# A Perceiver, RWKV and switched-attention layer on one core: the low parts of the transposed context blocks made by adding transfers instead of by VectorE and GpSimd

## The chip, the core and the metric

The kernel runs on one core of a Trainium2 chip. The metric is the device time of one execution in microseconds (us). TensorE (PE in the rows) multiplies matrices, and its weight loads are listed as PEld; VectorE is DVE, ScalarE is ACT, GpSimd is POOL, and SyncE (SP) issues transfers. Each engine works through its own list of instructions in order and waits on semaphores for the others; 16 DMA engines move data between device memory and the on-chip memory (SBUF). TensorE accumulates into eight banks of PSUM.

## The reference

Inputs are x (2 x 128 x 512) and a context (2 x 2048 x 512), all float32. There are three layers, each added to x after a layer norm. The first holds the change: self-attention, then a cross-attention over the context, then a small feed-forward part. The cross-attention is

```
Q = x @ Wq;  K, V = (context @ Wk, context @ Wv)
energy = einsum('bqd,bkd->bqk', Q, K)            # b = 2, q = 128, k = 2048
lengths = sum(energy[:, 0] != 0)                 # keys beyond the length are masked
score = softmax(where(pad, -inf, energy) / sqrt(32))
out = einsum('bqk,bkd->bqd', score, V)
```

The second layer is one RWKV-7 block with a state that starts at zero (eight projections, sigmoid and softplus gates, group norm); the third is an eight-head attention with experts chosen by the top two of five gates.

## The kernel before

The kernel never forms K and V of the whole context. It folds Wk into the query (`Q @ Wk.T`, called k2) and multiplies the result by the transposed context, and it gathers the context with the softmax weights before it multiplies by Wv (v2). So the context is read twice: in eight transposed blocks `ct00` to `ct13` (batch 0 or 1, quarter 0 to 3 of the keys) for the energies, and in eight plain blocks `c00` to `c13` for the gather. Each block is 128 x 2048 float32, 1 MB.

These sixteen products are made from rounded operands (float32r, which TensorE reads faster) in three passes so that precision is kept: each operand is split into a rounded high part and a low part, which is the remainder, and the product is high x high + low x high + high x low. The function `three` does that with 12 matmuls of 128 x 512 a block. The split of a context block has these steps:

- SyncE loads the block into its place in `ring` (`fetch`, L306). There are nine places for all weights and blocks (PLACE, L24), and a new block waits until the product that read the old one is done.
- ScalarE (`split`, L1333) writes the high part into one of the three places 9 to 11. Block i takes the place of block i - 3, so its split waits until the product of that block is done.
- VectorE (`low`, L806) writes block minus high part over the block for columns 0 to 1407, and GpSimd (`low`, L1578) does so for the other 640 columns. The two work at the same time, each after the split.
- TensorE waits in `three` for the split and both low parts.

The lists of all engines are written out by hand. TensorE's order around the change is: the self-attention of both batches, the query products q2(0) and k2(0), then scores(0,0), (0,1), (0,2), (0,3), q2(1), a count of nonzero energies, k2(1), scores(1,0), two transposes of the softmax weights of batch 0, scores(1,1) and (1,2), two more transposes, scores(1,3), and then the four gathers of batch 0 and the four of batch 1. VectorE counts nonzero energies after each of the scores (`nonzero`, L887) and makes the masked maximum of a batch (`maxima`, L900) once its count is through TensorE (`length2`, L892). GpSimd's list also holds the power -0.5 of every layer norm (`deviation`, L1574), on which the norm on VectorE waits; two of these, for x1 of both batches, stand between the low parts of `ct02` and `ct03`.

Of the kernel before, what the change touches and what calls it, by code (L numbers as in the profile page):

```python
# [7 lines left out]
ALU = mybir.AluOpType  # L8
ACT = mybir.ActivationFunctionType
# [5 lines left out]
BLOCKS = ["q1", "k1", "v1", "q2", "k2", *[f"ct{b}{n}" for b in range(2) for n in range(4)],  # L15
          "c00", "c01", "c02", "c03", "v2", "c10", "c11", "c12", "c13", "f1", "f2",
          "rk", "ra", "rw", "rr", "rv", "rg", "ro", "rf", "fg", "fq", "fk", "fo"]
# [6 lines left out]
PLACE = {n: i % 9 for i, n in enumerate(BLOCKS[:24])}  # L24
# [3 lines left out]
SPLITS = [f"ct{b}{n}" for b in range(2) for n in range(4)] + [f"c{b}{n}" for b in range(2) for n in range(4)]  # L28
# [47 lines left out]
def build(nc, blocks, xin, vecs, cols, out):  # L76
    with ExitStack() as ctx:
# [3 lines left out]
        def sem(name):  # L81
            return ctx.enter_context(nc.semaphore(name))
# [7 lines left out]
        ring = view("ring", [128, PLACES, 2048], F32, at)  # L90
        ring_r = view("ring_r", [128, PLACES, 2048], F32R, at)
# [54 lines left out]
        def high(name):  # L146
            return 9 + SPLITS.index(name) % 3
# [60 lines left out]
        def flags(name, *orders):  # L208
            return [Flag(sem(f"{name}{b}"), orders[b if len(orders) > 1 else 0]) for b in range(2)]
# [3 lines left out]
        four = ["0", "1", "2", "3"]  # L213

        s_place = [sem(f"s_place{p}") for p in range(PLACES)]
        s_x = [sem("s_x0"), sem("s_x1")]
        s_cols, s_bc0, s_bc1, s_bc2 = (sem(n) for n in ("s_cols", "s_bc0", "s_bc1", "s_bc2"))
        s_y = [sem("s_y0"), sem("s_y1")]
# [2 lines left out]
        own_v = Steps(sem("dve_steps"))  # L221
        var = flags("var_and_eps", LNS)
        normed = flags("normed", LNS)
        split_low = Flag(sem("split_low_dve"), SPLITS)
        energy_in = flags("energy_read", ["n1", "len1", "nb1", "max1", "pT"])
        k1_in = flags("k1_in", ["k1"])
        turned_v = Flag(sem("x_turned_dve"), ["x1"])
# [18 lines left out]
                      ["q1", "v1", "q2", "k2", "pc", "relu", "k", "th", "w", "r", "v", "g"])  # L246
        exped = flags("exped", ["e1"] + four)
        split_high = Flag(sem("split_high"), SPLITS)
        p_high = flags("p_high", four)
        mixed = flags("mixed", ["a", "k", "v", "r", "g"], ["w", "g"])  # L250
        sq_a = flags("squared", ["vc"], ["kx", "a", "wexp", "y"])
# [8 lines left out]
        own_g = Steps(sem("pool_steps"))  # L260
        const = Flag(sem("constants"), ["mhalf", "ident", "ones", "kidx", "causal", "kof", "top", "wbias", "tri", "sel"])
        rstd = flags("rstd", LNS)
        split_lowg = Flag(sem("split_low_pool"), SPLITS)
        x2b_g = flags("x2b", ["x2b"])
        mixed_g = Flag(sem("mixed_pool"), ["w", "g"])
        rk_g = flags("rwkv_pool", ["sb", "sc", "pv"], ["kx", "c2", "a", "c3", "sb", "w", "c1", "pv", "rs"])
# [107 lines left out]
        def _(eng):  # L374
# [36 lines left out]
            def three(o_, xs, name, first, last):  # L411

                s.wait_ge(*split_high.at(name))
                s.wait_ge(*split_low.at(name))
                s.wait_ge(*split_lowg.at(name))
                ws = [ring_r[:, p, :].rearrange("p (c n) -> p c n", c=4) for p in (high(name), PLACE[name])]
                pairs = [(xs[0], ws[0]), (xs[1], ws[0]), (xs[0], ws[1])]
                for n, (x, w) in enumerate(pairs):
                    for c in range(4):
                        i = mm(o_, x(c), w[:, c, :], first and n == c == 0, last and n == 2 and c == 3)  # L420
                return i
# [359 lines left out]
        def _(eng):  # L781
# [24 lines left out]
            def low(name):  # L806
                p = PLACE[name]
                s.wait_ge(*split_high.at(name))
                v.tensor_tensor(ring_r[:, p, 0:CUT], ring[:, p, 0:CUT], ring_r[:, high(name), 0:CUT],  # L809
                                ALU.subtract).then_inc(*split_low.inc(name))  # L810
# [340 lines left out]
            weigh(0)  # L1151
            pT(0)
            k1_out(1)
            low("ct00")
            low("ct01")
            add1(0)
            energies(1)
            low("ct02")
            norm1(0)
            lengths(1)  # L1160
            masked(1)
# [5 lines left out]
            norm1(1)  # L1167
            k2_split(0)
            nonzero(0, 0)
            low("ct03")  # L1170
            nonzero(0, 1)
            low("ct10")
            nonzero(0, 2)
            low("ct11")
            nonzero(0, 3)
            low("ct12")
            length2(0)
            maxima(0)
            k2_split(1)
# [1 line left out]
            guard(0, len2[0])  # L1181
            weigh2(0)
            nonzero(1, 0)
            low("ct13")
            p_split(0, 0)
            p_split(0, 1)
            nonzero(1, 1)
# [146 lines left out]
        def _(eng):  # L1334
            s = Waits(eng)

            def act(o, x, func, **kw):
                return a.activation(o, x, func, **kw)  # L1338
# [9 lines left out]
            def split(name):  # L1348
                i = SPLITS.index(name)
                s.wait_ge(*loaded(name))  # L1350
                if i > 2:
                    s.wait_ge(*used(SPLITS[i - 3]))
                act(ring_r[:, high(name), :], ring[:, PLACE[name], :], ACT.Copy).then_inc(*split_high.inc(name))

            def exp1(b):
                em = slots[:, 16, 256 + b * 128:384 + b * 128]
# [214 lines left out]
        def _(eng):  # L1571
# [6 lines left out]
            def low(name):  # L1578
                p = PLACE[name]
                s.wait_ge(*split_high.at(name))  # L1580
                g.tensor_tensor(ring_r[:, p, CUT:], ring[:, p, CUT:], ring_r[:, high(name), CUT:],  # L1581
                                ALU.subtract).then_inc(*split_lowg.inc(name))

            def mul(o, x, y, flag, name, op=ALU.mult):
                g.tensor_tensor(o, x, y, op).then_inc(*flag.inc(name))  # L1585

# [22 lines left out]
            g.affine_select(out=tri[:, :, :], in_=tri[:, :, :], compare_op=ALU.is_gt, fill=0.0, base=0,  # L1609
                            pattern=[[1, 5], [-1, 5]], channel_multiplier=0).then_inc(*const.inc("tri"))  # L1610
            deviation(1, "x")
            low("ct00")
            low("ct01")
            low("ct02")
            deviation(0, "x1")
            deviation(1, "x1")
            for name in SPLITS[3:]:
                low(name)
            for b in range(2):
                deviation(b, "x2")  # L1620
# [130 lines left out]
```

## Time and profile before

| | before |
|---|---|
| median of 3 runs | 277.52 us (277.33 to 278.31) |
| span of the profiled execution, first to last instruction | 275.8 us |
| mean granted clock of TensorE in it | 0.937 of full speed |
| busy: TensorE, its weight loads | 237.3 us (86%), 167.4 us (61%) |
| busy: VectorE, ScalarE, GpSimd | 177.9 us (64%), 88.3 us (32%), 99.6 us (36%) |

The profile gives no duration of the profiled execution other than its span; the part outside the span is taken as the difference to the median, 1.7 us. The table's shares are means over the whole span. The work in question lies between 23 and 123 us of it.

### The profile page before, as it was taken

How to read it: one execution, taken by the hardware profiler on the slowest of the kernel's cores; microseconds unless marked ns; L12 is line 12 of the kernel's file. 1: busy time of each engine (PE TensorE's matmuls, PEld its weight loads, DVE VectorE, ACT ScalarE, POOL GpSimd, SP SyncE). 2: the span in 40 equal slices, each digit the busy share in tenths (PEclk: the TensorE clock that was granted, in tenths of full speed). 3: DMA queues.
4: the chain of work that ended last, by engine and by line, in shares of the span. 5: the costliest groups of instructions: out<-in, count | busy, mean ns of one | idle time of the engine just before them, and what ended most of it. 6: DMA issues, size and time to landing. Idle time of an engine off the chain costs nothing.

```text
span 275.8 us, 3044 instructions
## 1 busy us (share of the span) xinstructions
PE 237.3 (86%) x1133; PEld 167.4 (61%) x1133; DVE 177.9 (64%) x327; ACT 88.3 (32%) x151; POOL 99.6 (36%) x82
## 2 busy tenths in 40 slices
PE   6999869899599949999989999970987599996995
PEld 5969458789488727677554444430433279895952
DVE  2236953379658999540747559599646869899360
ACT  2106410363467538412014545410202302321110
POOL 4002810088039933530402024886215236160000
PEclk9999968999899997999999999997799979999579
DMA  6999991002799991009800797000000000000001
GB/s 269 394 421 450 409 422 76 1 0 101 289 429 421 421 424 51 0 11 392 358 2 1 221 421 311 1 0 0 0 0 0 2 0 0 4 0 0 2 37 40
DMA packets 6350, 43.98 MB, mean 159 GB/s; under 512 B 832, under 2 KB 832, under 8 KB 1472
## 3 DMA queue, kind: packets, MB, share of 16 engines
q1 hardware_dynamic: 6336, 43.80, 39.1%
q8 instruction: 9, 0.15, 0.2%
q14 instruction: 5, 0.04, 0.1%
HBM read 43.27 MB, written 0.52 MB: 159 GB/s over the span
## 4 chain that ended last, share of the span: by engine, by line
PE 54%; DVE 29%; POOL 5%; issue 5%; ACT 4%; DMA 1%; DVEq 0%; POOLq 0%; ACTq 0%
PE psum L378 50%; PE psum L382 4%; DVE ring_r L809 4%; ACT slots L1338 3%; POOL small L1576 3%; DVE slots L1078 3%; DVE slots L904 2%; POOL slots L1585 2%; DVE slots L1081 2%; DVE small L785 1%; DVE slots L978 1%; DVE slots L909 1%; DMA slots<-xin 1%; DVE small L1091 1%; DVE slots L998 1%
## 5 line engine op out<-in xcount | busy, mean ns | idle before, releaser
L378 PE MATMUL psum<-ring,slots 128*128 128x512 f32 (+3 forms) x228 | 96.2, 576 | 4.4 <-ACT slots L1338 4.4
L378 PEld LDWEIGHTS psum<-ring,slots 128*128 128x128 f32 (+1 forms) x228 | 43.2, 209 | 48.7 <-issue 41.5
L1338 ACT ACTIVATE slots<-psum 128x512 f32<-128x512 f32 (+3 forms) x51 | 27.7, 552 | 123.6 <-PE psum L378 76.2
L1581 POOL TENSOR_TENSOR ring_r<-ring,ring_r 128x640 fp32r<-128x640 f32 x16 | 41.5, 2608 | 48.5 <-ACT ring_r L1338 48.5
L378 PE MATMUL psum<-slots,ring 128*128 128x128 f32 x448 | 54.7, 283 | 2.9 <-ACT slots L1338 2.4
L378 PEld LDWEIGHTS psum<-slots,ring 128*128 128x128 f32 x448 | 53.5, 199 | 5.1 <-ACT slots L1338 3.4
L378 PE MATMUL psum<-ring_r,slots_r 128*128 128x512 f32 x192 | 48.4, 410 | 3.4 <-issue 3.4
L378 PEld LDWEIGHTS psum<-ring_r,slots_r 128*128 128x128 f32 x192 | 37.1, 196 | 12.6 <-issue 4.9
L1576 POOL TENSOR_TENSOR small<-small,mhalf 128x1 f32<-128x1 f32 x16 | 14.9, 932 | 62.2 <-DVE small L789 62.2
L1338 ACT ACTIVATE ring_r<-ring 128x2048 fp32r<-128x2048 f32 (+1 forms) x17 | 31.7, 1864 | 14.2 <-PE psum L378 12.6
L382 PE MATMUL psum<-ident,slots 128*128 128x128 f32 x104 | 17.1, 298 | 19.5 <-DVE slots L1274 7.9
L809 DVE TENSOR_TENSOR ring_r<-ring,ring_r 128x1408 fp32r<-128x1408 f32 x16 | 29.8, 1871 | 6.1 <-ACT ring_r L1338 6.1
L382 PEld LDWEIGHTS psum<-ident,slots 128*128 128x128 f32 x104 | 13.2, 152 | 26.4 <-DVE slots L1274 8.7
L1338 ACT ACTIVATE slots<-slots,small 128x128 f32<-128x128 f32 (+1 forms) x30 | 12.7, 476 | 11.8 <-DVE small L915 6.5
L785 DVE BATCH_NORM_STATS2 small<-slots 128x6 f32<-128x512 f32 x16 | 11.1, 693 | 5.0 <-DMA slots<-xin 4.6
L1585 POOL TENSOR_TENSOR slots<-slots 128x512 f32<-128x512 f32 x7 | 9.3, 1335 | 13.7 <-ACT slots L1338 13.5
L1585 POOL TENSOR_TENSOR slots<-slots,bc 128x512 f32<-128x512 f32 x7 | 9.7, 1392 | 4.5 <-DVE slots L998 2.6
L1338 ACT ACTIVATE slots_r<-psum 128x512 fp32r<-128x512 f32 (+1 forms) x11 | 5.9, 558 | 16.7 <-PE psum L378 8.5
L803 DVE SCALAR_TENSOR_TENSOR slots<-slots,small,bc 128x512 f32<-128x512 f32 x10 | 7.5, 752 | 5.7 <-POOL small L1576 5.7
L935 DVE SCALAR_TENSOR_TENSOR slots<-psum,small,slots 128x512 f32<-128x512 f32 x2 | 1.5, 750 | 12.2 <-PE psum L378 12.2
L378 PE MATMUL psum<-slots 64*128 64x128 f32 (+2 forms) x68 | 8.7, 303 | 0.6 <-DVE slots L864 0.4
L978 DVE SCALAR_TENSOR_TENSOR slots<-slots,colv 128x128 f32<-128x128 f32 x16 | 6.5, 458 | 3.1 <-PE psum L378 3.0
(149 smaller groups left out, 211.1 us busy)
## 6 DMA issues: line engine op xcount, KB each, us to landing
ring<-blocks SPq DMA_DIRECT2D x36, 1024.0 KB, 10.2
bc<-vecs SPq DMA_DIRECT2D x1, 3072.0 KB, 28.4
bc<-vecs SPq DMA_DIRECT2D x1, 1280.0 KB, 8.1
slots<-xin SPq DMA_DIRECT2D x2, 256.0 KB, 3.9
bc<-vecs SPq DMA_DIRECT2D x1, 512.0 KB, 9.9
y<-slots SPq DMA_DIRECT2D x2, 256.0 KB, 2.0
colv<-cols SPq DMA_DIRECT2D x1, 14.0 KB, 8.7
```

Of the source, the lines that this page charges most:

```text
L378: return t.matmul(o_, l, r, start=first, stop=last)
L382: i = t.transpose(o_[:, c * 128:(c + 1) * 128], x[:, c * 128:(c + 1) * 128], ident[:, :])
L785: v.bn_stats(st[b], x).then_inc(*own_v.inc())
L803: v.scalar_tensor_tensor(out=o, in0=tmp, scalar=rs[b], in1=vec(bname), op0=ALU.mult, op1=ALU.add).then_inc(*normed[b].inc(name))
L809: v.tensor_tensor(ring_r[:, p, 0:CUT], ring[:, p, 0:CUT], ring_r[:, high(name), 0:CUT], ALU.subtract).then_inc(*split_low.inc(name))
L904: v.tensor_scalar(PT[b][:, at_], kidx[:, :], low4[b][:, n:n + 1], NEG, ALU.is_ge, ALU.mult).then_inc(*own_v.inc())
L978: i = v.scalar_tensor_tensor(out=dst[:, c, :], in0=bcols(T10, 1)[:, c, :], scalar=colv[:, 4 * k + c:4 * k + c + 1], in1=bcols(T8, 1)[:, c, ...
L1078: v.tensor_tensor(heads(N4[b] if first else Y[b]), x_, w_, ALU.mult).then_inc(*own_v.inc())
L1338: return a.activation(o, x, func, **kw)
L1576: g.tensor_tensor(rs[b], ve[b], mhalf[:, 0:1], ALU.pow).then_inc(*rstd[b].inc(name))
L1581: g.tensor_tensor(ring_r[:, p, CUT:], ring[:, p, CUT:], ring_r[:, high(name), CUT:], ALU.subtract).then_inc(*split_lowg.inc(name))
L1585: g.tensor_tensor(o, x, y, op).then_inc(*flag.inc(name))
```

## The change

For the eight transposed blocks the remainder is no longer computed by VectorE and GpSimd. ScalarE runs a second activation over the block in place: it overwrites the block with minus its rounded value. Then GpSimd's queue issues a transfer of the same block from device memory onto that place with an add as its write operation, so that block + (-rounded) is left there. TensorE waits for that transfer (16 increments of a semaphore for each block) instead of the two low parts. The eight `low` calls go from VectorE's list and the eight from GpSimd's; the plain blocks c00 to c13 are split as before.

```
+        s_added = {n: sem(f"s_added_{n}") for n in SPLITS[:8]}
...
                 s.wait_ge(*split_high.at(name))
-                s.wait_ge(*split_low.at(name))
-                s.wait_ge(*split_lowg.at(name))
+                if name.startswith("ct"):
+                    s.wait_ge(s_added[name], 16)
+                else:
+                    s.wait_ge(*split_low.at(name))
+                    s.wait_ge(*split_lowg.at(name))
...
             k1_out(1)
-            low("ct00")
-            low("ct01")
             add1(0)
             energies(1)
-            low("ct02")
             norm1(0)
...
                 act(ring_r[:, high(name), :], ring[:, PLACE[name], :], ACT.Copy).then_inc(*split_high.inc(name))
+                if i < 8:
+                    s.wait_ge(*split_high.at(name))
+                    act(ring_r[:, PLACE[name], :], ring[:, PLACE[name], :], ACT.Copy, scale=-1.0).then_inc(
+                        *minus_high.inc(name))
...
+            def add_block(name):
+
+                s.wait_ge(*minus_high.at(name))
+                g.dma_start(ring_r[:, PLACE[name], :], blocks[BLOCKS.index(name), :, :], accum_op=ALU.add).then_inc(
+                    s_added[name], 16)
...
             deviation(1, "x")
-            low("ct00")
-            low("ct01")
-            low("ct02")
+            add_block("ct00")
+            add_block("ct01")
+            add_block("ct02")
             deviation(0, "x1")
             deviation(1, "x1")
-            for name in SPLITS[3:]:
+            add_block("ct03")
+            add_block("ct10")
+            add_block("ct11")
+            add_block("ct12")
+            add_block("ct13")
+            for name in SPLITS[8:]:
                 low(name)
```

The diff also takes the calls of `low` for ct03 and ct10 to ct13 from between the counts on VectorE.

ScalarE's list, from the exponent of batch 0's self-attention on; `ring_r<-ring 128x2048` is a pass over a whole context block. Before:

```order
4 L1338 ACTIVATE slots,small<-slots,small 128x128
5 L1338 ACTIVATE ring_r<-ring 128x2048 x2
6 L1338 ACTIVATE slots<-psum 128x4x128
7 L1338 ACTIVATE ring_r<-ring 128x2048
8 L1338 ACTIVATE slots<-psum 128x512
```

And after the change:

```order
4 L1335 ACTIVATE slots,small<-slots,small 128x128
5 L1335 ACTIVATE ring_r<-ring 128x2048 x4
6 L1335 ACTIVATE slots<-psum 128x4x128
7 L1335 ACTIVATE ring_r<-ring 128x2048 x2
8 L1335 ACTIVATE slots<-psum 128x512
```

The eviction of q1 of batch 1 (row 6) now stands behind four passes instead of two. Further down the same list, from the split of ct03 to the first evictions of softmax weights (`slots_r<-psum 128x512`), before:

```order
14 L1338 ACTIVATE ring_r<-ring 128x2048 x4
15 L1338 ACTIVATE slots<-psum 128x4x128
16 L1338 ACTIVATE slots_r<-psum 128x4x128
17 L1338 ACTIVATE slots,small<-slots,small 128x512 x4
18 L1338 ACTIVATE ring_r<-ring 128x2048
19 L1338 ACTIVATE slots_r<-psum 128x512 x2
```

And after the change:

```order
14 L1335 ACTIVATE ring_r<-ring 128x2048 x8
15 L1335 ACTIVATE slots<-psum 128x4x128
16 L1335 ACTIVATE slots_r<-psum 128x4x128
17 L1335 ACTIVATE slots,small<-slots,small 128x512 x4
18 L1335 ACTIVATE ring_r<-ring 128x2048 x2
19 L1335 ACTIVATE slots_r<-psum 128x512 x2
```

The split of ct13 (row 18) is now two passes, ahead of the evictions of row 19. GpSimd's list from the second deviation on, before:

```order
21 L1576 TENSOR_TENSOR small<-small,mhalf 128x1
22 L1581 TENSOR_TENSOR ring_r<-ring,ring_r 128x640 x3
23 L1576 TENSOR_TENSOR small<-small,mhalf 128x1 x2
24 L1581 TENSOR_TENSOR ring_r<-ring,ring_r 128x640 x13
25 L1576 TENSOR_TENSOR small<-small,mhalf 128x1
```

And after the change:

```order
21 L1577 TENSOR_TENSOR small<-small,mhalf 128x1
22 L1588 DMA ring_r<-blocks 128x2048 x3
23 L1577 TENSOR_TENSOR small<-small,mhalf 128x1 x2
24 L1588 DMA ring_r<-blocks 128x2048 x5
25 L1582 TENSOR_TENSOR ring_r<-ring,ring_r 128x640 x8
26 L1577 TENSOR_TENSOR small<-small,mhalf 128x1
```

The deviations of x1 now stand behind three issues of adding transfers, each of which waits for ScalarE's second pass.

## Rows read from the trace of the kernel before

**Rows 1.** The page's first two parts, whole span.
```profile
PE 237.3 (86%) x1133; PEld 167.4 (61%) x1133; DVE 177.9 (64%) x327; ACT 88.3 (32%) x151; POOL 99.6 (36%) x82
...
PEclk9999968999899997999999999997799979999579
```

**Rows 2.** The chain that ended last: start us, us, what.
```profile
50.98 14.82 PE psum L378 x80
...
70.96 2.36 issue
73.32 4.58 PE psum L378 x12
...
78.77 5.50 PE psum L378 x24
...
94.57 1.73 DVE slots L904
...
102.54 0.16 DVE small L915
```

**Rows 3.** Timeline, 54:62: start us, us, engine, what [idle before <-releaser].
```profile
53.79 8.43 PE L378 MATMUL psum<-ring_r,slots_r 128*128 128x512 f32 x36
...
54.05 1.92 ACT L1338 ACTIVATE ring_r<-ring 128x2048 fp32r<-128x2048 f32 x1 [2.49 <-PE psum L378]
...
56.00 1.62 DVE L809 TENSOR_TENSOR ring_r<-ring,ring_r 128x1408 fp32r<-128x1408 f32 x1 [1.33 <-ACT ring_r L1338]
56.05 8.82 POOL L1581 TENSOR_TENSOR ring_r<-ring,ring_r 128x640 fp32r<-128x640 f32 x3 [7.10 <-ACT ring_r L1338]
```

**Rows 4.** The low parts' durations in ns, min/median/max.
```profile
L1581 POOL TENSOR_TENSOR ring_r<-ring,ring_r x16: 1543/2960/3028, 25.0 to 112.3; 128x640 fp32r<-128x640 f32 x16
```

**Rows 5.** All 36 block transfers, from issue to landing.
```profile
DMA to landing us min/median/max: 4.6/10.2/30.4
```

**Rows 6.** Issues by line, 0 to 50 us: KB each, median us to landing.
```profile
ring<-blocks SPq DMA_DIRECT2D x12, 1024.0 KB, 13.5
```

**Rows 7.** Stretches: us, busy us of each engine, PEclk, DMA share, GB/s.
```profile
38.00:41.00 3.00, 2.75 (x13) 2.75 (x14) 0.74 (x4) 0.58 (x3) 0.00 (x0) 0.50 1.00 415
...
57.00:60.00 3.00, 3.00 (x15) 2.34 (x14) 2.51 (x4) 2.20 (x2) 3.00 (x2) 1.00 0.00 0
...
78.00:84.00 6.00, 6.00 (x32) 5.06 (x30) 4.46 (x8) 4.80 (x4) 3.39 (x2) 1.00 1.01 426
```

**Rows 8.** Timeline of SyncE, its first issue of a block: start us, us.
```profile
1.23 0.42 SPq L312 DMA_DIRECT2D ring<-blocks  x1
```

**Rows 9.** Timeline, 20 to 41 us.
```profile
27.81 0.60 ACT L1338 ACTIVATE slots<-psum 128x512 f32<-128x512 f32 x1 [0.38 <-PE psum L378]
...
32.81 2.73 POOL L1576 TENSOR_TENSOR small<-small,mhalf 128x1 f32<-128x1 f32 x1 [0.47 <-DVE small L789]
...
36.45 1.11 PE L382 MATMUL psum<-ident,slots 128*128 128x128 f32 x4 [3.09 <-DVE slots L803]
...
38.25 6.08 PE L378 MATMUL psum<-slots,ring 128*128 128x128 f32 x32 [0.69 <-ACT slots L1338]
```

**Rows 10.** Timeline, 62 to 73 us, from q2(1) to scores(1,0).
```profile
62.06 3.73 PE L378 MATMUL psum<-slots,ring 128*128 128x128 f32 x32
...
66.46 1.32 DVE L897 TENSOR_SCALAR small<-kof,small 128x4 f32<-128x4 f32 x1
...
72.53 0.68 DVE L884 TENSOR_TENSOR slots_r<-psum,slots_r 128x512 fp32r<-128x512 f32 x1
```

**Rows 11.** Timeline, 77 to 88 us, around scores(1,3).
```profile
77.99 1.92 ACT L1338 ACTIVATE ring_r<-ring 128x2048 fp32r<-128x2048 f32 x1 [1.75 <-PE psum L378]
...
83.63 5.95 POOL L1581 TENSOR_TENSOR ring_r<-ring,ring_r 128x640 fp32r<-128x640 f32 x2 [0.62 <-ACT ring_r L1338]
84.10 1.03 PE L382 MATMUL psum<-ident,slots 128*128 128x128 f32 x8
...
84.89 5.73 PE L378 MATMUL psum<-ring_r,slots_r 128*128 128x512 f32 x24
```

More of the change, by code:

```diff
@@ L223, in build @@
         normed = flags("normed", LNS)
-        split_low = Flag(sem("split_low_dve"), SPLITS)
+        split_low = Flag(sem("split_low_dve"), SPLITS[8:])
         energy_in = flags("energy_read", ["n1", "len1", "nb1", "max1", "pT"])
@@ L248, in build @@
         split_high = Flag(sem("split_high"), SPLITS)
+        minus_high = Flag(sem("minus_high"), SPLITS[:8])
         p_high = flags("p_high", four)
@@ L262, in build @@
         rstd = flags("rstd", LNS)
-        split_lowg = Flag(sem("split_low_pool"), SPLITS)
+        split_lowg = Flag(sem("split_low_pool"), SPLITS[8:])
         x2b_g = flags("x2b", ["x2b"])
@@ L1169, in _ @@
             nonzero(0, 0)
-            low("ct03")
             nonzero(0, 1)
-            low("ct10")
             nonzero(0, 2)
-            low("ct11")
             nonzero(0, 3)
-            low("ct12")
             length2(0)
@@ L1183, in _ @@
             nonzero(1, 0)
-            low("ct13")
             p_split(0, 0)
```

## The prediction

> **What bounds the kernel now.** I read the page first, then the chain that ended last, then the timeline around each of the eight transposed blocks, then stretches with the granted clock. The shares say that TensorE is busy 86% of the span and VectorE 64% [rows 1]. The chain says more: from 50.98 to 65.8 us it is TensorE without a break (scores of batch 0, then q2 of batch 1), and again from 77.9 to 84.3; only later, from 84 to 103 us, does VectorE hold it [rows 2]. So in the stretch in which the eight blocks are used, what counts is whether a block is ready when TensorE comes to it. VectorE and GpSimd have slack there, and time taken off them is worth something only where the chain runs through them. The reader should also see in rows 1 that among the first 17 clock digits (6.9 us each) there are three clear drops; each follows an idle gap of TensorE of 3 us or more.
>
> **Part 1: what is removed.** Eight low parts on VectorE (1.62 us each at best, as the row at 56.00) and eight on GpSimd, of 1.54 to 3.03 us, median 2.96 [rows 3, 4]. That is at least 13 us of VectorE and between 12 and 24 us of GpSimd. Nearly all of it lies beside TensorE's work. It is on the chain, or lengthens what is on it, at two places only, named below.
>
> **Part 2: what is added.** For each block a second ScalarE pass of 1.92 us [rows 3], then an issue on GpSimd's queue, then the landing of an adding transfer. These three come one after the other, where the two low parts ran side by side behind the first pass. The trace has no adding transfer. Let D be the time from the end of the second pass to its landing. From below: the fastest landing of a plain 1 MB block is 4.6 us [rows 5]; an adding one cannot well be shorter, as it moves the same bytes and reads the place too. From above: a block in the first 50 us, which queues behind others, takes 13.5 us in the median [rows 6]; with 2.5 us more for the second read (1 MB at 421 GB/s [rows 7]) that is 16 us. I take, for a quiet moment, 4.6 + 2.5 + 0.4 for the issue (SyncE's first took 0.42 us [rows 8]) = 7.5 us, near the lower row because the DMA engines are idle at 57 to 60 us [rows 7]. For ct13, which is added in the midst of the load stream (DMA share 1.01 [rows 7]), half the rate would make it 12.5; I take 10.
>
> The Trainium skill, "Collectives: The Full Stack" (why AllGather, ReduceScatter and AllReduce differ), holds that an adding transfer is slowed by its two source reads and not by the addition, and gives 62.28 against 32.35 GB/s, a factor of 1.93. By that a 2.5 us move would be an estimated 4.8 us, which is D = 7.3 in place of 7.5; no run here shows it yet.
>
> **Part 3: the first three blocks (23 to 41 us).** They are not needed before 50.98 us, so even at 16 us their adding transfers are covered: ScalarE runs 23.0 to 26.9 for ct00, to 30.7 for ct01, then the eviction of q1 of batch 1 (27.81 before [rows 9]), then ct02 until 35.2; 35.2 + 16 = 51.2. But two things are queued behind. The eviction comes 2.9 us later, and so do e1 and v1 of batch 1 on TensorE, which have slack to about 36 us. And GpSimd's deviation of x1 of batch 0 stands behind the issue of ct02's add, which waits for 35.2: it ends about 37.2 instead of 35.5, although VectorE, freed of two low parts, would have been ready for it some 2 us sooner than before. It was 2.73 us long, since it shared its time with a low part of VectorE, and would now be about 1 [rows 9]. The norm, and q2(0) behind it, come 1.7 us later. Against that TensorE's gap ahead of them shrinks from 3.1 to about 2 us, because v1 of batch 1 now fills it. If the clock then stays up, q2(0) takes 3.8 instead of 6.08 us (the row at 62.06 is the same work at full clock [rows 9, 10]) and the transposes 0.7 instead of 1.11: -2.7. Bounds -1.0 and +1.7; I take +0.5.
>
> **Part 4: ct03.** Its high part can be written only when scores(0,0) is done: 54.05 to 55.97. Before, both low parts were there at 59.0 (56.05 + 2.96), and TensorE reached scores(0,3) at 53.79 + 2 x 2.81 = 59.4, just in time [rows 3]. Now the second pass ends at 57.9 and the block is there at 57.9 + 7.5 = 65.4: a stall of 6.0 us. The gap lowers the clock: scores(1,0), which follows a gap of 3.0 us, took 4.58 us against 2.81, so +1.8 for scores(0,3) [rows 2, 3]. Two things come back. Behind q2(1) the chain runs over the maxima of batch 0 on VectorE; there the 128x4 instruction of L897 took 1.32 us while GpSimd still worked on a low part, and without it about 0.2: -1.1 [rows 10]. And since k2(1) keeps its length while VectorE comes sooner, the gap ahead of scores(1,0) falls from 3.0 to 1.7 us; I count the clock as kept, -1.8. Sum of the part: 6.0 + 1.8 - 1.1 - 1.8 = +4.9 (bounds at D = 4.6 and 16: +0.2 without the drop of the clock, and +13.4). ct10, ct11 and ct12 are added 15 us and more before they are needed, and cost nothing.
>
> **Part 5: ct13.** Its high part waits for scores(1,0), which ends at 77.9. Passes 77.99 to 81.8 [rows 11]; landing at 81.8 + 10 = 91.8. TensorE wants it at 84.9 [rows 11]: 6.9 us, and again +1.8 for the clock, +8.7 (bounds at D = 4.6 and 16: +1.5 and +14.7). The evictions of batch 0's weights come 1.9 us later behind the second pass, and with them the low parts of the weights on VectorE, but the next transposes wait only at 83.9 and are just met. Behind scores(1,3) the order is as before: split of c02, low parts of c02 and c03, maxima of batch 1. GpSimd has the same low parts there, so the slowed instructions of L904 (1.73 us at 94.57 [rows 2]) stay. From there the delay is carried to the end unchanged.
>
> **Sum.** 0.5 + 4.9 + 8.7 = 14.1 us on a span of 275.8; with 1.7 us outside the span the median goes from 277.5 to 291.6. I say 291.
>
> **Rivals.** *The transfers are hidden and the freed engines pay.* VectorE and GpSimd slow each other where both work: a GpSimd low part takes 1.54 us at its shortest and 2.96 in the median [rows 4]. If the adds land in 4.6 us, part 3 gives -1.0, ct03 +0.2, ct13 +1.5, and if GpSimd, no longer late with ct13, is out of the way of batch 1's maxima (94.5 to 102.5 us, 8.0 long, against 67.8 to 72.5, or 4.7, for the same work in batch 0 [rows 2, 10]), another -3.3: -2.6, 274.9 us, faster. It decides below D = 5.9 or so for both blocks. Against it: a landing equal to the very fastest plain one, from a queue that has not been used in this kernel.
>
> *The adding transfer is slow*, 16 us: 0.5 + 13.4 + 14.7 = 28.6, 306 us. For it: 16384 elements an engine have to pass whatever adds them, and nothing in the trace says how fast.
>
> *The issue on GpSimd is long.* If it takes 3 us, as a low part beside VectorE does [rows 4], instead of 0.4, all three places slip by 2.6: 14.1 + 7.8 = 21.9, 299 us. The two engines wait for each other in the rows above. The Trainium skill, "SBUF — State Buffer" (the "DVE blocks DMA" trap), says the same of transfers issued from GpSimd: their descriptors cannot be written while a VectorE instruction holds the shared port pair. By that rule the sum would move toward this rival only where VectorE works long, and at 57.9 and 81.8 it now has only short instructions.
>
> *The change adds up to nothing*: D near 6 at both places, 277.5.
>
> **Chances.** Forecast 0.50 (283 to 297), long issue 0.15, slow adder 0.22, hidden 0.08, nothing 0.05. The range of 282 to 307 leaves out the last two and a tail of about 0.06 above. Half a percent (1.4 us) is about what a measurement of this kernel can tell from no change: faster 0.08, same 0.05, slower 0.87.
>
> **What would show it.** In the changed profile: ScalarE has eight more 1.92 us passes; TensorE idles ahead of scores(0,3), with a releaser that is a transfer, for about 6 us, and ahead of scores(1,3) for about 7; the clock falls behind each; the first three blocks cause no stall; q2(0) starts near 40 us; L897 of batch 0 takes 0.2 us. I am wrong if there is no idle time ahead of scores(0,3), if the adds take under 6 us or over 16 from the end of the pass, or if ct10 to ct12 stall TensorE too.

## The result, and the profile after

| | before | after |
|---|---|---|
| median | 277.42 us (275.56 to 278.31, 4 runs) | 295.26 us (293.17 to 296.38, 4 runs) |
| ratio, 95% interval | | 1.0639 (1.0563 to 1.0714), slower |
| profiled execution | span 275.8 us | 296.38 us, span 294.6 us |

The changed kernel is slower by 17.8 us. The forecast was 291 us, with a range of 282 to 307. In all tables the medians are of all runs, and the ratios leave out the runs that took over 1.5% longer than the fastest of the same kernel. The page after, in the same order of engines as [rows 1], with the groups that the change touches (line engine op, tile, count | busy, mean ns | idle before them and what ended most of it; q0 is the queue of GpSimd's transfers, with packets, MB and share of the 16 engines):

```profile
PE 241.7 (82%) x1133; PEld 169.3 (57%) x1133; DVE 160.6 (55%) x319; ACT 102.8 (35%) x159; POOL 84.3 (29%) x82
...
PEclk9999999978999579689999999999589979999579
...
q0 software_dynamic: 1152, 8.39, 14.1%
...
L380 PE MATMUL psum<-ring_r,slots_r 128*128 128x512 f32 x192 | 52.4, 431 | 19.3 <-DMA ring_r<-blocks 17.1
...
L1335 ACT ACTIVATE ring_r<-ring 128x2048 fp32r<-128x2048 f32 (+1 forms) x25 | 46.6, 1874 | 27.0 <-PE psum L380 25.2
...
L1588 POOL DMA_DIRECT2D ring_r<-blocks x8 | 7.2, 894 | 62.1 <-ACT ring_r L1335 62.1
...
ring_r<-blocks POOLq DMA_DIRECT2D x8, 1024.0 KB, 12.8
```

The change does what it says: VectorE is 17.3 us less busy, GpSimd 15.3 less, ScalarE 14.5 more. The fourth row holds the answer: of 19.3 us that TensorE idled ahead of these products, a transfer into `ring_r` ended 17.1. The chain that ended last (start us, us, what), beside [rows 2]:

```profile
53.26 1.93 ACT ring_r L1335
55.20 1.92 ACT ring_r L1335
...
57.41 7.99 DMA ring_r<-blocks
65.54 8.14 PE psum L380 x44
73.69 10.53 DMA ring<-blocks
84.25 1.93 ACT ring_r L1335
86.20 1.92 ACT ring_r L1335
88.40 12.38 DMA ring_r<-blocks
100.92 5.47 PE psum L380 x12
...
113.05 1.73 DVE slots L909
```

Where [rows 2] had TensorE without a break, the chain now leaves it twice: two passes, the issue, the landing of the adding transfer, once for ct03 and once for ct13, the second time behind the plain load of ct13 itself (10.53 us). The timeline (start us, us, engine, what, idle before and its releaser), beside [rows 3, 9, 10, 11]:

```profile
39.68 3.84 PE L380 MATMUL psum<-slots,ring 128*128 128x128 f32 x32 [0.69 <-ACT slots L1335]
...
50.17 5.71 PE L380 MATMUL psum<-ring_r,slots_r 128*128 128x512 f32 x24 [0.47 <-issue]
...
56.27 3.01 PE L380 MATMUL psum<-ring_r,slots_r 128*128 128x512 f32 x12 [0.40 <-DMA ring_r<-blocks]
57.41 0.89 POOL L1588 DMA_DIRECT2D ring_r<-blocks  x1 [9.29 <-ACT ring_r L1335]
65.54 4.55 PE L380 MATMUL psum<-ring_r,slots_r 128*128 128x512 f32 x12 [6.26 <-DMA ring_r<-blocks]
74.21 0.23 DVE L902 TENSOR_SCALAR small<-kof,small 128x4 f32<-128x4 f32 x1
79.98 3.01 PE L380 MATMUL psum<-ring_r,slots_r 128*128 128x512 f32 x12 [1.56 <-ACT slots_r L1335]
84.25 3.86 ACT L1335 ACTIVATE ring_r<-ring 128x2048 fp32r<-128x2048 f32 x2 [1.34 <-DMA ring<-blocks]
87.15 2.97 PE L380 MATMUL psum<-ring_r,slots_r 128*128 128x512 f32 x12 [0.52 <-DMA ring_r<-blocks]
88.40 0.86 POOL L1588 DMA_DIRECT2D ring_r<-blocks  x1 [13.20 <-ACT ring_r L1335]
100.92 8.33 PE L380 MATMUL psum<-ring_r,slots_r 128*128 128x512 f32 x24 [9.93 <-DMA ring_r<-blocks]
```

Read beside before, this gives the shift of each point. The difference of two neighbours is what the stretch between them costs.

| point | before | after | shift |
|---|---|---|---|
| k1 of batch 1, ahead of any changed work | 20.25 | 22.26 | +2.0 |
| scores(0,0) starts | 50.98 | 50.17 | -0.8 |
| scores(0,2) starts | 56.6 | 56.27 | -0.3 |
| scores(0,3) starts | 59.4 | 65.54 | +6.1 |
| scores(0,3) ends | 62.2 | 70.1 | +7.9 |
| scores(1,0) starts | 73.32 | 79.98 | +6.7 |
| scores(1,0) ends | 77.9 | 83.0 | +5.1 |
| scores(1,3) starts | 84.9 | 100.92 | +16.0 |
| scores(1,3) ends | 87.7 | 106.4 | +18.7 |
| last instruction | 275.8 | 294.6 | +18.8 |

The first row is not the change's. The first projections took 8.85 us in this execution against 7.41 before, and the same happens in kernels that leave this stretch alone (8.84 us in the one with three low parts later, 7.41 in the one with two). Up to 11 us the matmuls come at 7 a us and then at 12, as if at half and at full clock, but the granted clock is shown as 1.00 in both stretches, so the reason stays open. By 56 us it is swallowed: scores(0,2) begins when ct02 has landed, at 56.1. In the kernel without ct13, which does not lose this time and starts scores(0,0) at 48.76, scores(0,2) begins at 56.05 as well. (59.4, 62.2, 56.6 and 87.7 are places inside a row of before, by 2.81 us for each block of 12 matmuls.)

The eight issues and landings, and three stretches with the busy us of PE, PEld, DVE, ACT and POOL, the granted clock, the DMA share and GB/s:

```profile
DMA to landing us min/median/max: 8.0/12.8/20.2
```

```profile
57.40:61.20 3.80, 1.88 (x9) 1.20 (x7) 0.69 (x2) 3.77 (x3) 0.93 (x2) 1.00 0.65 123
61.20:65.40 4.20, 0.00 (x0) 0.00 (x0) 0.00 (x0) 3.37 (x2) 1.32 (x2) 0.61 0.96 197
...
70.00:73.70 3.70, 3.70 (x34) 3.58 (x32) 0.69 (x2) 3.48 (x2) 0.00 (x0) 1.00 1.04 215
...
100.90:106.40 5.50, 5.48 (x13) 4.34 (x14) 0.00 (x0) 0.00 (x0) 0.00 (x0) 0.50 1.01 426
```

When the transfer of ct03 is issued, the last plain loads take about one more microsecond, and it lands 8.0 us after its issue. From 70.0 to 73.7 us the engines are as full as with plain loads and move 215 GB/s, where a plain stream moves 426. The last row is scores(1,3) at half clock behind the idle time.

### The profile page after: what moved, and what is told of

Read it like the earlier page. It is cut to its first block, busy times and chain, and to the rows that moved or that the text cites. A ratio compares the mean times of both kernels' runs of the same rounds, so it can differ in the third digit from the quotient of the medians.

```text
span 294.6 us, 3042 instructions
## 1 busy us (share of the span) xinstructions
PE 241.7 (82%) x1133; PEld 169.3 (57%) x1133; DVE 160.6 (55%) x319; ACT 102.8 (35%) x159; POOL 84.3 (29%) x82
## 3 DMA queue, kind: packets, MB, share of 16 engines
q0 software_dynamic: 1152, 8.39, 14.1%
## 4 chain that ended last, share of the span: by engine, by line
PE 45%; DVE 23%; DMA 11%; ACT 10%; POOL 5%; issue 4%; DVEq 0%; POOLq 0%; ACTq 0%
PE psum L380 42%; ACT ring_r L1335 7%; DMA ring_r<-blocks 7%; PE psum L384 4%; DMA ring<-blocks 4%; ACT slots L1335 3%; DVE slots L1083 2%; POOL small L1577 2%; POOL slots L1592 2%; DVE slots L1086 1%; DVE slots L909 1%; DVE small L790 1%; DVE ring_r L814 1%; DVE slots L983 1%; DVE slots L914 1%
## 5 line engine op out<-in xcount | busy, mean ns | idle before, releaser
L380 PE MATMUL psum<-ring_r,slots_r 128*128 128x512 f32 x192 | 52.4, 431 | 19.3 <-DMA ring_r<-blocks 17.1
L380 PEld LDWEIGHTS psum<-ring_r,slots_r 128*128 128x128 f32 x192 | 39.3, 210 | 30.4 <-issue 19.3
L380 PE MATMUL psum<-slots,ring 128*128 128x128 f32 x448 | 53.9, 281 | 3.1 <-ACT slots L1335 2.7
L1335 ACT ACTIVATE ring_r<-ring 128x2048 fp32r<-128x2048 f32 (+1 forms) x25 | 46.6, 1874 | 27.0 <-PE psum L380 25.2
L384 PE MATMUL psum<-ident,slots 128*128 128x128 f32 x104 | 17.3, 304 | 16.5 <-DVE slots L1271 7.9
L1577 POOL TENSOR_TENSOR small<-small,mhalf 128x1 f32<-128x1 f32 x16 | 13.1, 817 | 59.5 <-DVE small L794 59.5
L1582 POOL TENSOR_TENSOR ring_r<-ring,ring_r 128x640 fp32r<-128x640 f32 x8 | 21.2, 2663 | 23.1 <-ACT ring_r L1335 23.0
L384 PEld LDWEIGHTS psum<-ident,slots 128*128 128x128 f32 x104 | 13.7, 156 | 23.1 <-DVE slots L1271 8.7
L1588 POOL DMA_DIRECT2D ring_r<-blocks x8 | 7.2, 894 | 62.1 <-ACT ring_r L1335 62.1
L894 DVE TENSOR_SCALAR_CACHE_REDUCE slots<-psum 1x512 f32<-1x512 f32 x8 | 5.4, 676 | 27.8 <-PE psum L380 27.8
L1335 ACT ACTIVATE slots<-slots,small 128x128 f32<-128x128 f32 (+1 forms) x30 | 12.7, 476 | 9.4 <-DVE small L920 4.1
L814 DVE TENSOR_TENSOR ring_r<-ring,ring_r 128x1408 fp32r<-128x1408 f32 x8 | 13.6, 1712 | 4.1 <-ACT ring_r L1335 4.1
L1592 POOL TENSOR_TENSOR slots<-slots 128x512 f32<-128x512 f32 x7 | 9.3, 1332 | 13.7 <-ACT slots L1335 13.5
## 6 DMA issues: line engine op xcount, KB each, us to landing
ring<-blocks SPq DMA_DIRECT2D x36, 1024.0 KB, 13.3
```

The costliest lines, as they stand in the source:

```text
L380: return t.matmul(o_, l, r, start=first, stop=last)
L384: i = t.transpose(o_[:, c * 128:(c + 1) * 128], x[:, c * 128:(c + 1) * 128], ident[:, :])
L894: v.tensor_scalar(PT[b][0:1, n * 512:(n + 1) * 512], psum[0:1, 4 * b + n, :], 0.0, 0.0, ALU.not_equal, ALU.add, accum_out=cnt4[b][0:1, n:n ...
L1577: g.tensor_tensor(rs[b], ve[b], mhalf[:, 0:1], ALU.pow).then_inc(*rstd[b].inc(name))
L1588: g.dma_start(ring_r[:, PLACE[name], :], blocks[BLOCKS.index(name), :, :], accum_op=ALU.add).then_inc(s_added[name], 16)
```

## The experiments

Each time is shown with the kernel before run on the same chip beside it. In kernels 1 to 6, 9 and 11 a list ADDED names the blocks that use the second pass and the adding transfer. The others keep `low` on both engines at its place of before.

### 1 to 4. The parts alone

```
+ADDED = ['ct03']                            # e1_only_ct03
+ADDED = ['ct13']                            # e2_only_ct13
+ADDED = SPLITS[:7]                          # e3_all_but_ct13
+ADDED = ['ct00', 'ct01', 'ct02']            # e4_first_three
...
             def low(name):
+                if name in ADDED:
+                    s.wait_ge(*minus_high.at(name))
+                    g.dma_start(ring_r[:, PLACE[name], :], blocks[BLOCKS.index(name), :, :], accum_op=ALU.add).then_inc(
+                        s_added[name], 16)
+                    return
```

> Only ct03 has the second pass and the adding transfer; the other seven blocks have their low parts on VectorE and GpSimd as before. Theory A (each of the two stalls has its own cause in the chain second pass, issue, landing): the DMA engines are idle at that point, so the transfer lands about 7 us after the pass; TensorE idles 5.5 us ahead of scores(0,3), +1.7 for the clock, less 1.6 for the smaller gap ahead of scores(1,0): 4.5 to 6 us slower than before, 282 to 284 us. Theory B (ct03 was late only because the three adds before it had clogged the DMA engines): D about 5, 1 to 3 us slower.

> Only ct13 has the second pass and the adding transfer. Theory A: it meets the load stream of the plain blocks, lands some 12 us after the pass, TensorE idles 8 to 9 us ahead of scores(1,3) and scores(1,3) runs at the low clock (+2.7): 10 to 12 us slower, 288 to 290. Theory B (in the changed kernel it was late because the seven adds before it had pushed the loads back, its own load among them): D about 8, 4 to 7 us slower, 282 to 285.

> The change for seven blocks, ct13 as before. Theory A (the two stalls add up): the time of the changed kernel less 9.9 us of idle time and 2.7 us of low clock: 282 to 284 us. Theory B (VectorE's chain behind scores(1,3) hides part of that stall): 286 us and more.

> Only ct00, ct01 and ct02 have the second pass and the adding transfer. Theory A: their transfers are covered; VectorE is free for the first norm, TensorE's gap ahead of q2(0) is too short to lower the clock, q2(0) takes 3.84 us instead of 6.08 and the rest of the path is 1.4 to 2 us later: 0 to 1.5 us faster than before. Theory B (they are not covered: with the load stream beside them ct02 lands 20 us after its issue): TensorE idles ahead of scores(0,2), 1 to 3 us slower.

| kernel | median | beside before (277.11) |
|---|---|---|
| only ct03 | 284.23 us | 1.0240 (1.0161 to 1.0320) |
| only ct13 | 290.83 us | 1.0549 (1.0464 to 1.0634) |
| all but ct13 | 284.37 us | 1.0265 (1.0198 to 1.0333) |
| the first three | 277.36 us | 1.0003 (0.9963 to 1.0044) |

Timeline of only ct03, scores(0,3) and scores(1,0), and its one landing:

```profile
66.11 4.76 PE L382 MATMUL psum<-ring_r,slots_r 128*128 128x512 f32 x12 [7.23 <-DMA ring_r<-blocks]
...
81.50 2.98 PE L382 MATMUL psum<-ring_r,slots_r 128*128 128x512 f32 x12 [2.54 <-issue]
```

```profile
DMA to landing us min/median/max: 8.3/8.3/8.3
```

Timeline of only ct13, scores(1,3) with the first gather, and its landing:

```profile
94.75 7.96 PE L382 MATMUL psum<-ring_r,slots_r 128*128 128x512 f32 x24 [10.50 <-DMA ring_r<-blocks]
```

```profile
DMA to landing us min/median/max: 13.3/13.3/13.3
```

The first three, q2(0) and scores(0,2) with (0,3):

```profile
39.64 3.84 PE L382 MATMUL psum<-slots,ring 128*128 128x128 f32 x32 [0.69 <-ACT slots L1347]
...
56.25 5.72 PE L382 MATMUL psum<-ring_r,slots_r 128*128 128x512 f32 x24 [0.40 <-DMA ring_r<-blocks]
```

One block alone costs 7.1 us (ct03) or 13.7 us (ct13), each with the stall and the lowered clock where the prediction put them. So the change has two prices and not eight. The two singles add up to 20.8 us, more than the 17.8 of all eight (by the ratios 21.8 against 17.7, with intervals of 2 us and more on either side of each single). In only ct13 the gap ahead of scores(1,0) is still 3.04 us and its matmuls take 4.43, where the changed kernel has 1.56 and 3.01. Only ct03 has 2.54 and 2.98: there the clock is kept with the other low parts in place. A gap of 1.56 is seen only in kernels where the low parts of all blocks up to there are off both engines. The first three alone make no difference that can be told, and the gain in the clock of q2(0) (3.84 us instead of 6.08) is real in their trace, as is a wait of 0.40 us for ct02, whose transfer took 20.2 us to land and so caps the gain. All but ct13 came out at the edge of what was expected. In its trace scores(0,0) starts at 48.76, 2.2 us sooner than before, but ct02 then holds up scores(0,2) by 1.60 us, and ct12's transfer makes scores(1,2) wait 1.95 us, and the clock falls behind that too (4.58 us for the 12 matmuls).

### 5. The same transfers without the addition

```
-                    g.dma_start(ring_r[:, PLACE[name], :], blocks[BLOCKS.index(name), :, :], accum_op=ALU.add)...
+                    g.dma_start(ring_r[:, PLACE[name], :], blocks[BLOCKS.index(name), :, :])...
```

> The changed kernel with all eight transfers from GpSimd's queue as plain copies instead of adds; the additions are left out, so the low parts are wrong and only the time is read. Theory A (an adding transfer moves at half the rate because it reads two sources; issue and fixed part are as in a copy): landing of ct03 falls from 8.0 to about 5.5 us and that of ct13 from 12.4 to 8 to 10, together 5 to 7 us less: 288 to 290 us. Theory B (what makes it long is the software queue of GpSimd itself): ct03 lands after 7.5 to 8 us as before and the time stays within 1.5 us of the changed kernel's 295.

290.57 us, 1.0428 (1.0337 to 1.0519) beside 276.91. By the ratios it is 11.9 us slower than before where the changed kernel is 17.7, so some 5.8 us less (4.7 by the medians). The issues (ns, min/median/max, from when to when) and landings:

```profile
L1594 POOL DMA_DIRECT2D ring_r<-blocks x8: 527/544/767, 29.5 to 87.0; - x8
```

```profile
DMA to landing us min/median/max: 5.0/7.8/13.1
```

And scores(0,3) and scores(1,3) in its timeline:

```profile
65.48 4.38 PE L382 MATMUL psum<-ring_r,slots_r 128*128 128x512 f32 x12 [4.07 <-ACT ring_r L1347]
...
96.23 7.10 PE L382 MATMUL psum<-ring_r,slots_r 128*128 128x512 f32 x24 [6.25 <-DMA ring_r<-blocks]
```

The fastest landing falls from 8.0 to 5.0 us and that of ct13 from 12.4 to 9.1, so the addition costs about 3 us at each place. The other 11.9 us of the price, two thirds of it, are there without it: pass, issue and transfer one after the other. The prediction counted 2.5 us for the addition, from the rate of a plain stream. The Trainium skill, "Collectives: The Full Stack" (why AllGather, ReduceScatter and AllReduce differ), says of ReduceScatter that the two source reads of its add, and not the addition itself, slow it by 1.93. The factor agrees with this case's trace: 421 GB/s [rows 7] over 215 is 1.96. That it comes from the second read and not from the addition is not shown here, as no run separates the two.

### 6 and 9. The load stream held back

```
+            s.wait_ge(s_added["ct13"], 16)
             fetch("v2")                     # e6_held_loads
...
+            s.wait_ge(s_added["ct13"], 16)
             fetch("c02")                    # e9_loads_out_of_the_way
```

> The changed kernel, but SyncE holds the load of v2 and all behind it until ct13's adding transfer has landed. Theory A (ct13's landing is 4 us longer than ct03's because of the load stream beside it): landing in 8 to 10 us instead of 12.4, 3 to 5 us less for the stall, if the held loads (c10 and later) still come in time: 290 to 293 us. Theory B (it is long by itself, or the loads already in flight are enough): no gain, and the plain blocks of batch 1 come late: 295 to 298.

> The changed kernel, but SyncE holds the loads of c02, c03, v2 and all behind them until ct13's adding transfer has landed (in the run before only v2 and later were held, and c00 to c03 were still in flight). Theory A (the load stream is what makes ct13's landing 4 us longer than ct03's): landing in 8 to 9.5 us instead of 12.4. The time itself may not fall, since c02 then comes in late for its split: 289 to 295 us. Theory B (it is long for another reason): the landing stays at 12 us or more and the time at 295 or above.

| kernel | median | ratio | ct13: issue to landing | idle ahead of scores(1,3) |
|---|---|---|---|---|
| changed | 295.26 us | 1.0639 | 12.4 us | 9.93 us |
| held before v2 | 292.85 us | 1.0581 (1.0512 to 1.0651) | 12.1 us | 7.49 us |
| held before c02 | 291.88 us | 1.0537 (1.0497 to 1.0576) | 10.1 us | 5.63 us |

The first hold was put too late: c00 to c03 had been issued by then and stood in the engines' queues, and the landing did not change. Its idle time is shorter for another reason: ct13's plain load landed in 8.1 us instead of 10.5, so the first pass came right behind scores(1,0), and 0.98 us more was spent waiting for ct12 just before. With two plain blocks fewer ahead the landing fell by 2.3 us. Timeline of the second, scores(1,3):

```profile
96.34 8.38 PE L383 MATMUL psum<-ring_r,slots_r 128*128 128x512 f32 x24 [5.63 <-DMA ring_r<-blocks]
```

The DMA view tells what moves meanwhile. Of the changed kernel, 88 to 95 us (q1 is the queue of the plain loads, q0 that of the adding transfers; packets, MB, share of the 16 engines):

```profile
q1 hardware_dynamic: 303, 2.21, 75.3%
q0 software_dynamic: 48, 0.39, 26.9%
```

In steps of 2 us all of 88 to 92 is plain (100 and 102%), though the adding transfer was issued at 88.40; its packets begin in 92 to 94 and have 61 to 88% of the engines until 98, with plain ones beside them. In the second hold the plain loads fall from 92% in 86 to 88 us to 5% in 88 to 90, and then it has the engines to itself. So the landing of ct13 is 4.4 us longer than ct03's because of plain loads ahead of and beside it, at least for the 2.3 us that the second hold took away. The other 2.1 us stay open: a kernel with no load in flight at the issue was not run. The medians say less than the idle times (the intervals of both holds overlap that of the changed kernel), since loads held back are wanted later; in the second a split waits 3.13 us for its load.

### 7. The second pass without the transfer

```
 act(ring_r[:, high(name), :], ring[:, PLACE[name], :], ACT.Copy).then_inc(*split_high.inc(name))
+if i < 8:
+    s.wait_ge(*split_high.at(name))
+    act(ring[:, PLACE[name], :], ring[:, PLACE[name], :], ACT.Copy).then_inc(*again.inc(name))
...
+if name.startswith("ct"):                   # in low, VectorE and GpSimd
+    s.wait_ge(*again.at(name))
```

> The kernel before with a second ScalarE pass over each of the eight transposed blocks (a float32 copy onto itself), and the low parts on VectorE and GpSimd behind it: the pass alone, no adding transfer. Theory A: ct03's low parts are ready at 59.0 + 1.9 = 60.9, TensorE wants them at 59.4: +1.5; ct13's at 84.9, just when TensorE comes; the eviction of q1 of batch 1 is 2.9 us later but has slack: 1 to 3 us slower, 278 to 280.5. Theory B (ScalarE's 15 us more are what costs, and the transfer little): 5 us slower or more.

291.39 us, 1.0508 (1.0428 to 1.0588) beside 276.91. That is 14 us where far less was expected, and the worst miss of the study. Timeline of scores(0,3), scores(1,0), GpSimd's low parts and the first gather:

```profile
62.85 4.18 PE L379 MATMUL psum<-ring_r,slots_r 128*128 128x512 f32 x12 [1.80 <-POOL ring_r L1589]
...
79.68 5.39 PE L379 MATMUL psum<-ring_r,slots_r 128*128 128x512 f32 x12 [4.13 <-issue]
...
89.17 13.33 POOL L1589 TENSOR_TENSOR ring_r<-ring,ring_r 128x640 fp32r<-128x640 f32 x4 [15.07 <-ACT ring L1341]
...
97.79 4.57 PE L379 MATMUL psum<-ring_r,slots_r 128*128 128x512 f32 x12 [2.30 <-POOL ring_r L1589]
```

The pass of 1.92 us is not paid once. It makes ct03 late (1.80 us and the clock), pushes the low parts of VectorE and GpSimd into the norm and the maxima that the chain runs over (4.13 us ahead of scores(1,0) against 3.00, and the clock), and makes the first gather wait for GpSimd. So the second pass, with the engines' low parts kept, costs nearly as much as the whole change; the change gets part of that back because it takes the low parts off both engines. The costs of its parts do not add up, and no single experiment gives one part's share.

### 11. Only ct10 and ct11

```
+ADDED = ['ct10', 'ct11']
```

> Only ct10 and ct11 have the second pass and the adding transfer: the two that are made longest before they are needed. Theory A (a covered transfer costs nothing, and freed engines give back about 1 us at L897 of batch 0): 0 to 2 us faster, 275 to 277. Theory B (ScalarE's two more passes and the transfers push ct12 or the loads back): 1 to 4 us slower.

279.81 us, 1.0105 (1.0062 to 1.0148) beside 277.20: slower by 2.6 us, though TensorE waits for neither block (landings 9.0 and 13.3 us). Timeline from ct10 to scores(1,0):

```profile
56.04 9.41 ACT L1347 ACTIVATE ring_r<-ring 128x2048 fp32r<-128x2048 f32 x5 [0.80 <-PE psum L382]
...
67.22 1.31 DVE L906 TENSOR_SCALAR small<-kof,small 128x4 f32<-128x4 f32 x1
...
74.08 5.31 PE L382 MATMUL psum<-ring_r,slots_r 128*128 128x512 f32 x12 [4.25 <-issue]
```

Five passes follow each other on ScalarE, and ct12, which its engines still split, comes last: its low part starts at 65.49, on VectorE and GpSimd, where the maxima of batch 0 want VectorE. The gap ahead of scores(1,0) grows from 3.0 to 4.25 us. "ct10, ct11 and ct12 cost nothing" looked at the transfers and not at ScalarE's queue. In the changed kernel ct12 has no low part, and this cost is not there.

### 8, 10 and 12. What the trace pointed to beside the change

In the kernel before, low parts hold up the norm of x1: on VectorE those of ct00 and ct01 run until 30.9 us, ahead of its first step, and on GpSimd its deviation takes 2.73 us beside a low part (0.88 in the changed kernel). The change gave that time away again, as its deviation waits for the issue of ct02's add; what it kept was the clock of q2(0). The time can be had in the kernel before, by the order alone:

```
             k1_out(1)                       # VectorE
-            low("ct00")
-            low("ct01")
             add1(0)
             energies(1)
-            low("ct02")
             norm1(0)
             lengths(1)
             masked(1)
             weigh(1)
+            low("ct00")                     # e8; in e10 and e12 ct00 stays where it was
+            low("ct01")
+            low("ct02")
...
             deviation(0, "x1")              # GpSimd, with the same low parts behind it
```

In the last kernel the split of k2 of batch 1 also goes ahead of the last of four maxima of batch 0:

```
             def maxima(b):
                 low_at = own_v.now()
                 for n in range(4):
+                    if b == 0 and n == 3:
+                        k2_split(1)
...
             maxima(0)
-            k2_split(1)
```

> The kernel before with the low parts of ct00 to ct02 moved in VectorE's list behind the first norm and the softmax weights of batch 1, and in GpSimd's list behind the deviation of x1 of batch 0; no second pass, no adding transfer. Theory A (what the first three blocks gain from the freed engines is the clock and the earlier norm): the norm of batch 0 comes 3 to 4 us sooner, TensorE's gap of 3 us is gone and q2(0) runs at full clock: 3 to 6 us faster, 271 to 274 us. Theory B (these engines' time is hidden there as elsewhere): within 1 us of before.

> The kernel before, without any adding transfer: only the low parts of ct01 and ct02 are moved, on VectorE behind the softmax weights of batch 1 and on GpSimd behind the deviation of x1 of batch 0; ct00's stays where VectorE waits for TensorE anyway. Theory A (the norm of batch 0 was held up by low parts, and the three-low version lost its gain since three of them, 4.7 us, did not fit ahead of pT of batch 1): q2(0) starts some 3 us sooner and at full clock, no stall of 4.3 us ahead of pv of batch 1: 3 to 6 us faster, 271 to 274 us. Theory B (two low parts still do not fit, or the time comes back at a later gap): within 1.5 us of before.

> The version with the low parts of ct01 and ct02 moved, and in addition the low part of k2 of batch 1 ahead of the last of the four maxima of batch 0 on VectorE, so that scores(1,0) starts some 1.1 us sooner. Theory A (an idle gap of TensorE of 3 us and more costs about 1.7 us more than its length, because the granted clock falls behind it, and one of 2 us does not): the gap ahead of scores(1,0) falls from 3.0 to about 1.9 us and its 12 matmuls take 2.8 to 3.0 us instead of 4.56: 2 to 3 us faster than that version, 270.5 to 272.5 us. Theory B (the clock falls behind a gap of 1.9 us as well, or the time comes back at the maxima of batch 1): 0 to 1.2 us faster, 272.8 to 274.

| kernel | median | ratio |
|---|---|---|
| three low parts later | 279.28 us | 1.0063 (1.0023 to 1.0103) |
| two later | 273.95 us | 0.9869 (0.9827 to 0.9911) |
| two later, split sooner | 271.79 us | 0.9829 (0.9770 to 0.9888) |

One of the six runs of the second took 595.62 us; it is unexplained and not in the ratio. Three low parts moved to one place only moved the wait, and by its ratio the kernel is 1.7 us slower (0.6 to 2.9) than before, where theory A had it faster and theory B within 1 us. Its timeline, VectorE and the next matmuls behind it:

```profile
40.23 4.69 DVE L809 TENSOR_TENSOR ring_r<-ring,ring_r 128x1408 fp32r<-128x1408 f32 x3
...
45.51 2.08 PE L378 MATMUL psum<-slots 128*128 128x512 f32 x2 [4.33 <-DVE slots L864]
```

With ct00 left in its place those matmuls wait 1.56 us, and all of scores(0) follows without a break. Timeline of two later, q2(0), scores(0,0) to (0,3), scores(1,0):

```profile
35.37 3.84 PE L378 MATMUL psum<-slots,ring 128*128 128x128 f32 x32 [0.69 <-ACT slots L1338]
...
47.04 11.22 PE L378 MATMUL psum<-ring_r,slots_r 128*128 128x512 f32 x48
...
69.38 4.56 PE L378 MATMUL psum<-ring_r,slots_r 128*128 128x512 f32 x12 [3.02 <-issue]
```

And scores(1,0) with the split sooner:

```profile
68.33 2.99 PE L378 MATMUL psum<-ring_r,slots_r 128*128 128x512 f32 x12 [1.80 <-issue]
```

A gap shorter by 1.2 us is worth 1.6 us more in the clock. The intervals of the last two kernels overlap, so that the last is better than the second rests on this row, and the ratios alone do not show it. It is the fastest version that was found, some 5 us below the kernel before.

## Why the prediction was right

The order of events was as foretold: two stalls, their places, their releasers and the clock behind them. Two of the signs of being wrong that it named did come, at small cost: ct12 stalled TensorE, and two of the first three adds took over 16 us from the end of the pass. The sum was 14.1 us and 17.8 came in the medians (18.8 in the two profiled executions, which the table splits up).

| step | predicted | measured (difference of shifts) |
|---|---|---|
| first three blocks (to the start of scores(0,2)) | +0.5 (bounds -1.0 and +1.7) | -0.3 |
| ct03: stall and clock | +7.8 | +8.2 |
| relief ahead of and in scores(1,0) | -2.9 | -2.8 |
| ct13: stall and clock | +8.7 | +13.6 |

- **First three blocks.** Right in mechanism and within the bounds, but not in sign: v1 fills the gap and the clock stays up, q2(0) took 3.84 us and began at 39.7, near the 40 foretold. "Even at 16 us they are covered" failed for ct02, which landed 20.2 us after its issue (ct01 after 17.0); it took back 0.40 us here and 1.60 in the kernel without ct13. By the first three alone the part is no difference, 1.0003.
- **ct03.** D was 8.3 us from the end of the pass (57.13 to 65.4) in place of 7.5: the issue took 0.89 us and not 0.4, the rest is the landing. Idle time 6.26 against 6.0, loss of clock 1.74 against 1.8.
- **Relief.** The 128x4 instruction took 0.23 us in place of 1.32, the gap fell from 3.00 to 1.56, and the clock held (3.01 us for 4.58). That is 1.4 and 1.6, as 1.1 and 1.8 were foretold.
- **ct13** is the term that was mis-sized, by 4.9 us. D was 12.7 us (88.12 to 100.79) and not 10, with plain blocks queued ahead of it; the value of 12.5 stood in the prediction as the case of half the rate. Two waits were missed: the plain load of ct13, now 10.53 us in a stretch in which adding transfers share the engines, came 1.3 us late for the first pass, and ct12's transfer held up scores(1,2) by 0.52. The second costs nothing here, since TensorE idles ahead of scores(1,3) anyway. "15 us and more before they are needed" was wrong for ct12: its first pass waits for scores(0,3), which the first stall had moved, and left 12.6 us, while it landed 13.0 us after its second pass. And the idle time of 9.93 us left the clock low for all 12 matmuls: 5.47 us, 2.7 over the usual and not 1.8. So the 4.9 us are 2.7 of D, 1.3 of the load and 0.9 of the clock.
- **From there to the end** nothing changed: the maxima of batch 1 start 18.5 us later at the same 1.73 us, as foretold, since GpSimd has the same low parts there.

Of the rivals, the hidden transfer is out: 8.0 us is the least, and all of it is on the chain. The slow adder (16 us) holds only for landings within the first loads, which are covered. The long issue is out as well: 0.85 to 1.07 us, and 0.5 for a plain one. The Trainium skill, "SBUF — State Buffer" (the "DVE blocks DMA" trap), would have the descriptors wait while a VectorE instruction holds the shared port pair; no issue here was long, and no run put one beside a long VectorE instruction on purpose, so the rule is not tried.

What stays open: the share of each part in the 17.8 us, since the parts do not add up, how much of ct13's landing is left with no other transfer in flight, and whether the adding transfer is slower by its second read or by the addition.

## What to carry to other kernels

When work that ran in two engines side by side is turned into a pass, an issue and a transfer in a row, look up which blocks have no slack between the release of their place and their use. Those paid here, two of eight, and each paid again in TensorE's clock. A block with slack can still cost something in the list of the engine that got the extra pass, as ct10 and ct11 alone did (2.6 us). Time taken off an engine is worth something only at the instruction of it that the chain runs through, and the trace shows which that is; it can often be had by order alone, as the two low parts moved behind a norm were worth more than any part of the change.

## What the runs showed that was not expected

- An adding transfer of 1 MB took 8.0 to 8.3 us with the DMA engines idle or nearly so and 12.4 to 13.3 in the load stream, a plain one from the same queue 5.0 and 9.1; its issue took 0.85 to 1.07 us against 0.53 to 0.77.
- A ScalarE pass of 1.92 us for each block, in the shadow of TensorE as it seemed, cost 14 us.
- Gaps of TensorE of 1.56, 1.80 and 2.54 us ahead of scores(1,0) left its clock up (3.0 us for the 12 matmuls), and after 2.70 to 4.25 us there it was down (4.4 to 5.4 us). But gaps of 1.80 us ahead of scores(0,3) in the second-pass kernel and 1.95 us ahead of scores(1,2) in the kernel without ct13 were followed by 4.18 and 4.58 us as well, so the length of the gap alone does not tell it.
